# Cross attention scores from two float32r parts in 64-row tiles, with one maximum instruction for two heads

## The chip, the cores and the metric

The kernel is one program on one core of a Trainium2 chip. The metric is device time in microseconds (us) of one execution; the kernel before took 3319.63 us (median of three runs, 3304.61 to 3321.81).

## What is computed

Two decoder layers on x of shape (4, 512, 512), each with a mixer, a second mixer or cross attention on a context of shape (4, 512, 256), and a feed-forward part, each followed by a layer norm. Only the second layer's cross attention is touched. For each of 4 batches and 32 heads of 16 channels it is

```python
q, k, v = x @ Wq, *split(ctx @ Wkv)            # 512 tokens, 512 keys
q, k = apply_axial_rope(q, pos), apply_axial_rope(k, pos)
out = softmax(q @ k.T * 16 ** -0.5) @ v
x = layernorm(x + out @ Wout + bout)
```

in float32 accuracy.

## The kernel before

The program runs six stages one after the other; all engines go through them in the same order and meet by semaphores. The fifth stage is `Cross` (L3013). It works in 16 units, a unit being 8 heads of one batch (one block of 128 channels). The engines run a software pipeline written out by hand: `iterations()` gives i, and in iteration i the scores that go to the exponential belong to unit i, the scores for the maximum to unit i+1, and the projections of q, k and v to unit i+3. Each iteration has 32 steps m.

**The scores.** A product of float32 accuracy is made out of bfloat16 parts. After the rotation each of q and k is cut into three bfloat16 parts (`rope`, L3229: seven instructions on POOL for q and again for k; unit 0's k is cut on DVE). The parts go to memory (`d_parts`) and come back stacked, channel by channel, on 96 partitions (`sp_stack`, L3159: one store and six loads for each of q and k), so that one bfloat16 matmul over 96 rows adds the six products that matter. `pe_max` (L3335) makes a 128x512 tile of scores with it and DVE takes the row maximum, negated (L3545: one TENSOR_REDUCE per tile, 32 per unit). The maxima of half a unit are cut into three parts (`dve_parts`, L3520, four instructions), turned by TensorE (`mT`, L3314), copied by ACT (L3427) and put by three DMAs into rows 96 to 98 of Q (`sp_rows`, L3142), against rows of ones in K. `pe_exp` (L3347, matmul at L3355) then makes the transposed scores with the maximum already taken off, over 99 rows, and ACT takes the exponential (L3446: 32 per unit, 128x512). `pe_values` (L3358, matmuls at L3368) multiplies four heads' exponentials by the values in four 32-column tiles of TensorE, eight times a unit, once for every four exponentials.

**The order on TensorE** (`pe_all`, L3374) is, for each step m: one score matmul for the exponential, one for the maximum, the values if m % 4 is 1, and then one job from a list. `misc(i)` (L3078) gives that list: Rq and Rk (the projections of q and k, L3300), V (the projection of v, L3306), mT (L3314), turn (the attention output turned back, L3319, emptied on DVE by L3505 and L3508), aT (L3324), and at the end or start of a batch y (the output projection, four jobs, L3332, added and measured on DVE at L3512 and L269), xT (x turned, four jobs, L3286) and ang (angles, L3290, whose sines ACT makes with its own table, L3411).

**PSUM** has 8 banks: two for the exponential's scores (`rexp`), three for the maximum's (`rmax`), one for the values (`rav`), two in turn for the jobs of the list (`ring`). A job waits until the bank that it takes has been emptied.

**Queues.** DVE does, in step m, the maximum of step m, and after it the job that TensorE had in step m-2; ACT the exponential of step m and after it the job of step m-1. All DMAs of the stage are issued by SP in the order of `sp_all` (L3176): in iteration i the swap of q's channels, the rows of maxima, the swap of k's, after the second iteration of a batch the four stores of the batch before, the stack of q, the rows of the next unit's first half, the stack of k.

Of the kernel before, what the change touches and what calls it, by code (L numbers as in the profile page):

```python
# [12 lines left out]
F32 = mybir.dt.float32  # L13
# [6 lines left out]
P = 128  # L20
# [2992 lines left out]
class Cross(Stage):  # L3013
# [4 lines left out]
    name, pool_works, unrolled = "cross", True, True  # L3018
    H, DH = 32, 16
    CC = 2  # L3020
    Q_PARTS = (0, 1, 0, 2, 1, 0)
    K_PARTS = (0, 0, 1, 0, 1, 2)
    N = 6 * 16
# [6 lines left out]
    ONES = 1.0 + 0x3F80 / 2 ** 23  # L3030
    ONCE = ("cross_weights", "cross_late", "cross_ones", "cross_identb", "cross_half_pi")
# [6 lines left out]
    def __init__(self, io, carve, ps, x_in, x_out):  # L3038
# [26 lines left out]
        s.rav = Ring("cross_av", ps, 5, 1, [((u, g), "act") for u in range(s.UNITS) for g in range(2)])  # L3065
# [12 lines left out]
    def misc(self, i):  # L3078
# [3 lines left out]
        starts = (i + s.AHEAD + 1) % C == 0 and nb < B  # L3082
        if s.unit(f) is not None and i != -1:
            yield 1, ("Rq", f)
        if s.unit(i) is not None:
            yield 3, ("mT", i, 1)
        if s.unit(i - 1) is not None:
            yield 5, ("turn", i - 1, 1)
        if s.unit(f) is not None and i != -1:
            yield 7, ("Rk", f)  # L3090
        if s.unit(i - 1) is not None:
            yield 11, ("aT", i - 1)
        if s.unit(f) is not None:
            yield 15, ("V", f)
        ends = s.unit(i - 1) is not None and i % C == 0
        if starts:
            yield 17, ("ang", nb)
# [932 lines left out]
```

## Time and profile before

| | |
|---|---|
| median of three runs | 3319.63 us |
| the profiled execution | 3316.54 us, its span 3314.8 us |
| PE (TensorE matmul) busy | 2716.1 us, 82% of the span |
| DVE busy | 1958.6 us, 59% |
| ACT busy | 1433.1 us, 43% |
| POOL busy | 1177.7 us, 36% |
| score matmuls for the exponential, L3355 | 512, 198.4 us busy |
| score matmuls for the maximum, L3341 | 512, 201.4 us busy |
| maxima, L3545 | 512, 330.3 us busy |
| exponentials, L3446 | 512, 287.8 us busy |

Busy time of PE is that of overlapping records: a score matmul is shown 0.38 us long, and the next starts 0.22 us after it. A float32 matmul is two records. "Idle before" an instruction is put down to the instruction that ended it. Iterations can be told in the trace by Rq, the eight records of L3300, which stand at step 1.

### The profile page before, as it was taken

Reading aid. Unit: us, or ns where it says so; the run is one execution under the profiler, and the core shown is the slowest. Engines: PE = TensorE matmul, PEld = TensorE weight load, DVE = VectorE, ACT = ScalarE, POOL = GpSimd, SP = SyncE. Lnnn points to the kernel's source line nnn. Section 1 sums busy time; section 2 is a strip of 40 time slices with the busy share of each in tenths; the row PEclk is TensorE's granted clock in tenths of the full one; section 3 lists DMA queues with packets and bytes.
Section 4 is the critical chain, followed back from the end, with each engine's and each line's share of the span. In section 5 each row is a group of like instructions: output and inputs, shape, how many; then the busy total and the mean of one; then the engine's idle time right before and its main releaser. Section 6 shows DMA issues by size and latency. Waiting matters only on the chain.

```text
span 3314.8 us, 50665 instructions
## 1 busy us (share of the span) xinstructions
PE 2716.1 (82%) x20138; PEld 1454.0 (44%) x20154; DVE 1958.6 (59%) x3064; ACT 1433.1 (43%) x2577; POOL 1177.7 (36%) x1118
## 2 busy tenths in 40 slices
PE   5788888876677676589988898888768989899787
PEld 3565656553223232268845444444433333333244
DVE  3323232333689889956526566656655657476477
ACT  3232333320545555423426262635315546465555
POOL 0443333441566666600023625243243424241000
PEclk8888888887888888799998999998879989899999
DMA  2222222130330304032332424243155435252301
GB/s 87 71 59 62 52 78 60 47 87 14 121 116 13 127 26 140 13 140 95 137 108 86 128 90 125 93 122 130 39 117 107 105 69 112 61 109 53 118 26 39
DMA packets 209370, 280.04 MB, mean 84 GB/s; under 512 B 84640, under 2 KB 111680, under 8 KB 208240
## 3 DMA queue, kind: packets, MB, share of 16 engines
q1 hardware_dynamic: 209136, 276.81, 29.4%
q8 instruction: 160, 2.62, 0.3%
q14 instruction: 74, 0.61, 0.1%
HBM read 192.08 MB, written 59.12 MB: 76 GB/s over the span
## 4 chain that ended last, share of the span: by engine, by line
PE 39%; DVE 10%; issue 5%; ACT 4%; POOL 2%; DMA 1%; SPq 0%; ACTq 0%; DVEq 0%; POOLq 0%
PE ps L236 7%; PE ps L3368 4%; PE ps L1846 4%; PE ps L1857 4%; PE ps L3355 4%; PE ps L3341 3%; PE ps L3300 3%; PE ps L3332 2%; PE ps L2512 1%; ACT arena L3446 1%; PE ps L2520 1%; DVE arena L2775 1%; DVE arena L1434 1%; DMA arena<-arena 1%; DVE arena L2773 1%
## 5 line engine op out<-in xcount | busy, mean ns | idle before, releaser
L236 PE MATMUL ps<-arena 128*128 128x512 f32 (+3 forms) x1280 | 473.6, 522 | 18.3 <-ACT arena L2612 6.1
L3545 DVE TENSOR_REDUCE arena<-ps 128x1 f32<-128x512 f32 x512 | 330.3, 685 | 229.2 <-PE ps L3341 227.8
L3446 ACT ACTIVATE arena<-ps 128x512 f32<-128x512 f32 x512 | 287.8, 597 | 283.2 <-PE ps L3355 279.7
L1466 POOL TENSOR_TENSOR arena<-arena 128x1024 f32<-128x1024 f32 x128 | 311.0, 2430 | 192.9 <-DVE arena L1458 192.9
L1482 PE MATMUL ps<-arena 128*128 128x512 f32 x512 | 267.2, 662 | 55.8 <-POOL arena L1466 55.5
L1458 DVE TENSOR_TENSOR_SCAN arena<-ps,arena 128x1024 f32<-128x1024 f32 x128 | 291.5, 2278 | 32.9 <-ACT ps L1449 32.9
L236 PEld LDWEIGHTS ps<-arena 128*128 128x128 f32 (+2 forms) x1296 | 193.2, 154 | 252.3 <-issue 172.9
L1449 ACT ACTIVATE ps<-arena 128x511 f32<-128x511 f32 x256 | 165.1, 679 | 188.3 <-DVE arena L1458 188.1
L576 POOL TENSOR_TENSOR arena<-arena 128x31 f32<-128x31 f32 (+15 forms) x217 | 130.1, 600 | 324.2 <-DMA arena<-d_a 307.8
L3355 PE MATMUL ps<-arena 99*128 99x512 bf16 x512 | 198.4, 390 | 45.3 <-ACT arena L3446 33.4
L3341 PE MATMUL ps<-arena 96*128 96x512 bf16 x512 | 201.4, 395 | 19.1 <-issue 15.4
L1482 PEld LDWEIGHTS ps<-arena 128*128 128x128 f32 x512 | 104.6, 213 | 212.2 <-issue 125.7
L2276 POOL TENSOR_TENSOR arena<-arena 128x512 f32<-128x512 f32 x64 | 66.7, 1042 | 286.5 <-DVE arena L2928 286.5
L2654 ACT ACTIVATE arena<-arena 128x128 f32<-128x128 f32 x512 | 155.4, 388 | 8.4 <-PE ps L2570 8.4
L1434 DVE TENSOR_TENSOR arena<-ps,arena 128x1024 f32<-128x1024 f32 x128 | 154.4, 1206 | 1.6 <-PE ps L1482 0.7
L3238 POOL TENSOR_TENSOR arena<-arena 128x512 f32<-128x512 f32 x31 | 39.4, 1271 | 307.6 <-ACT arena L3419 307.4
L1084 DVE TENSOR_TENSOR arena<-ps,arena 128x256 f32<-128x256 f32 x120 | 51.0, 425 | 157.7 <-PE ps L777 157.7
L3368 PE MATMUL ps<-arena 128*32 128x512 f32 x1024 | 141.6, 626 | 1.0 <-ACT arena L3446 1.0
L3355 PEld LDWEIGHTS ps<-arena 99*128 99x128 bf16 x512 | 49.8, 98 | 197.4 <-ACT arena L3446 142.8
L1846 PE MATMUL ps<-sign,sign 128*128 128x512 f32 x512 | 122.5, 401 | 6.5 <-issue 6.5
L578 POOL TENSOR_TENSOR arena<-arena 128x31 f32<-128x31 f32 (+15 forms) x217 | 116.6, 537 | 17.0
L1857 PE MATMUL ps<-sign,sign 128*128 128x512 f32 x512 | 121.5, 396 | 0.0
(352 smaller groups left out, 5254.1 us busy)
## 6 DMA issues: line engine op xcount, KB each, us to landing
arena<-d_bc SPq DMA_DIRECT2D x32, 1024.0 KB, 5.7
arena<-d_x SPq DMA_DIRECT2D x24, 1024.0 KB, 6.8
arena<-d_parts SPq DMA_DIRECT2D x192, 128.0 KB, 4.6
d_x<-arena SPq DMA_DIRECT2D x64, 256.0 KB, 2.5
arena<-arena SPq DMA_DIRECT2D x128, 128.0 KB, 2.1
arena<-in_D_wlm SPq DMA_DIRECT2D x12, 1024.0 KB, 6.6
d_parts<-arena SPq DMA_DIRECT2D x32, 384.0 KB, 2.4
d_signs<-arena SPq DMA_DIRECT2D x32, 256.0 KB, 2.1
```

Of the source, the lines that this page charges most:

```text
L236: ins = pe.e.matmul(ps[:m, :n], lhsT(k), rhs(k), start=(k == 0), stop=(k == chunks - 1))
L1434: dve.e.tensor_tensor(s.h[:, i % s.HS].rearrange("p (w l) -> p w l", w=s.W), spread(s.ps[:, s.DTU, :], 1, s.W), s.bc[:, turn % s.SLOTS, 0] ...
L1458: dve.e.tensor_tensor_scan(h, s.dA[:, i % 2].rearrange("p w l -> p (w l)"), h, 0.0, ALU.mult, ALU.add).then_inc(*dve.up("scan_scanned"))
L1466: pool.e.tensor_tensor(h, h, s.bc[:, turn % s.SLOTS, 1], ALU.mult).then_inc(*pool.up("scan_hC"))
L1482: ins = pe.e.matmul(y, s.ident, s.h[:, i % s.HS, w * L:(w + 1) * L], start=False, stop=last)
L1846: ins = e.matmul(ps, s.up[m // 4][:, k, m % 4 * P:(m % 4 + 1) * P], s.xp[i][:, k, :], start=(k == i == 0), stop=(k == C - 1 and i == 1))
L1857: ins = e.matmul(ps, s.hp[i][:, m, t * P:(t + 1) * P], s.down[:, m, :], start=(m == i == 0), stop=(m == s.FC - 1 and i == 1))
L3341: pe.e.matmul(s.rmax.bank((u, m)), s.Qs[:s.N, slot, h, t * P:(t + 1) * P], s.Ks[:s.N, slot, h, :], start=True, stop=True).then_inc(*s.rmax ...
L3355: pe.e.matmul(s.rexp.bank((u, i)), s.Ks[:s.N + 3, slot, s.G * g + j, k * P:(k + 1) * P], s.Qs[:s.N + 3, slot, s.G * g + j, :], start=True, ...
L3368: ins = e.matmul(ps[32 * j:32 * j + 32, :], s.V[:, u % s.SLOTS, k, s.G * g + j, :], s.E[:, k % 2, j, :], start=(k == 0), stop=(k == s.KEYS ...
L3446: act.e.activation(s.E[:, k % 2, j], s.rexp.bank((u, i)), ACT.Exp).then_inc(*s.rexp.empty(act, (u, i)))
L3545: dve.e.tensor_reduce(s.mx[:, u % 2, t, h:h + 1], s.rmax.bank((u, m)), AX.X, ALU.max, negate=True).then_inc(*s.rmax.empty(dve, (u, m)))
```

## The change

- q and k are cut into two float32r parts instead of three bfloat16 parts (two instructions instead of four), and three products are added: 48 rows instead of 96. Even heads lie on partitions 0 to 47, odd heads on 64 to 111. Each load of `sp_stack` becomes two (six in all, as before, of the same 128 KB, in pieces of 2 KB instead of 1 KB); the store has 512 KB instead of 384 KB.
- A score matmul reads 48 rows (50 with the maxima) from row 0 or row 64, in float32r. TensorE issues two for the exponential, then two for the maximum, then the values, then the jobs.
- The two for the maximum fill two neighbouring banks and one TENSOR_REDUCE takes the maxima of both: 16 per unit, of 1024 columns.
- `rmax` has two slots of two banks, and `ring` one bank instead of two.
- The maxima are cut into two parts, by two instructions instead of four, and put in place by two DMAs instead of three. The rows of ones come from two DMAs ahead of SP's first swap instead of from four memsets on DVE.
- The jobs get other steps: xT at 9, 13, 23, 25; y at 27 and 29 and, in the next iteration, at 9 and 11 (after the last unit at 13, 15, 17, 19). The norm's square root moves from step 2 to 18, its scaling from step 4 to 20.

```diff
-    Q_PARTS = (0, 1, 0, 2, 1, 0)
-    K_PARTS = (0, 0, 1, 0, 1, 2)
-    N = 6 * 16
+    Q_PARTS = (0, 0, 1)
+    K_PARTS = (0, 1, 0)
+    N = 3 * 16
...
-        s.ring = Ring("cross", ps, 6, 2, [(name, s.EMPTIES[name[0]]) for i in s.iterations() for _, name in s.misc(i)])
+        s.ring = Ring("cross", ps, 7, 1, [(name, s.EMPTIES[name[0]]) for i in s.iterations() for _, name in s.misc(i)])
...
-        s.rmax = Ring("cross_max", ps, 2, 3, [((u, m), "dve") for u in range(s.UNITS) for m in range(s.STEPS)])
+        s.rmax = Ring("cross_max", ps, 2, 2, [((u, m), "dve") for u in range(s.UNITS) for m in range(0, s.STEPS, 2)], 2)
...
+            items += [(3, ("mT", i, 1)), (21, ("turn", i, 0))]
...
+            items += [(5, ("turn", i - 1, 1)), (13 if i > C and i % C == 1 else 11, ("aT", i - 1))]
...
+            items += [(at, ("xT", nb, t)) for t, at in enumerate((9, 13, 23, 25))]
+        ends = range(T) if i == s.UNITS else (0, 1) if i > 0 and i % C == 0 else (2, 3) if i > C and i % C == 1 else ()
+        at = (13, 15, 17, 19) if i == s.UNITS else (27, 29, 9, 11)
...
         for a, part in enumerate((s.Q_PARTS, s.K_PARTS)[w]):
-            sp.e.dma_start(dst[16 * a:16 * a + 16], d[:, :, part, :].rearrange("h d l -> d h l")).then_inc(*sp.up(f"cross_stack_{'qk'[w]}", 16))
+            for p in range(2):
+                at = 64 * p + 16 * a
+                sp.e.dma_start(dst[at:at + 16].bitcast(F32), d[p::2, :, part, :].rearrange("h d l -> d h l")).then_inc(*sp.up(f"cross_stack_{'qk'[w]}", 16))
...
-        hi, mid, lo = (s.parts[:, w, a] for a in range(3))
+        hi, lo = (s.parts[:, w, a] for a in range(2))
         e.tensor_copy(hi, s.m1[:, w]).then_inc(*eng.up_step("cross"))
         eng.e.wait_ge(*eng.at_step("cross"))
-        e.tensor_tensor(s.rest[:, w], s.m1[:, w], hi, ALU.subtract).then_inc(*eng.up_step("cross"))
-        eng.e.wait_ge(*eng.at_step("cross"))
-        e.tensor_copy(mid, s.rest[:, w]).then_inc(*eng.up_step("cross"))
-        eng.e.wait_ge(*eng.at_step("cross"))
-        e.tensor_tensor(lo, s.rest[:, w], mid, ALU.subtract).then_inc(*eng.up(f"cross_parts_{n}"))
+        e.tensor_tensor(lo, s.m1[:, w], hi.bitcast(F32), ALU.subtract).then_inc(*eng.up(f"cross_parts_{n}"))
...
         pe.e.wait_ge(*s.rmax.at_free(pe, (u, m)))
-        pe.e.matmul(s.rmax.bank((u, m)), s.Qs[:s.N, slot, h, t * P:(t + 1) * P], s.Ks[:s.N, slot, h, :],
-                    start=True, stop=True).then_inc(*s.rmax.fill(pe, (u, m)))
+        for p in range(2):
+            rows = slice(64 * p, 64 * p + s.N)
+            ins = pe.e.matmul(s.rmax.bank((u, m))[:, p, :], s.Qs[rows, slot, hh, t * P:(t + 1) * P], s.Ks[rows, slot, hh, :], start=True, stop=True)
+        ins.then_inc(*s.rmax.fill(pe, (u, m)))
...
-        pe.e.matmul(s.rexp.bank((u, i)), s.Ks[:s.N + 3, slot, s.G * g + j, k * P:(k + 1) * P], s.Qs[:s.N + 3, slot, s.G * g + j, :],
+        hh, p = 2 * g + j // 2, j % 2
+        rows = slice(64 * p, 64 * p + s.N + 2)
+        pe.e.matmul(s.rexp.bank((u, i)), s.Ks[rows, slot, hh, k * P:(k + 1) * P], s.Qs[rows, slot, hh, :],
...
-            for m in range(s.STEPS):
+            for m in range(1, s.STEPS, 2):
                 if s.unit(i) is not None:
+                    s.pe_exp(pe, i, m - 1)
                     s.pe_exp(pe, i, m)
                 if s.unit(i + 1) is not None:
-                    s.pe_max(pe, i + 1, m)
+                    s.pe_max(pe, i + 1, m - 1)
...
-                    dve.e.tensor_reduce(s.mx[:, u % 2, t, h:h + 1], s.rmax.bank((u, m)), AX.X, ALU.max, negate=True).then_inc(*s.rmax.empty(dve, (u, m)))
+                    if m % 2 == 0:
+                        h, t = m // (2 * T) * 2, m // 2 % T
+                        dve.e.wait_ge(*s.rmax.at_filled(dve, (u, m)))
+                        dve.e.tensor_reduce(s.mx[:, u % 2, t, h:h + 2], s.rmax.bank((u, m)), AX.X, ALU.max, negate=True).then_inc(*s.rmax.empty(dve, (u, m)))
```

## Rows read from the trace of the kernel before

**Rows 1.** Busy time by stretch, the whole stage: us, PE, PEld, DVE, ACT, POOL, clock, DMA

```profile
2414.83:3141.35 726.52, 636.94 (x3016) 237.80 (x3016) 441.06 (x806) 371.81 (x684) 244.86 (x234) 0.93 0.44 96
```

**Rows 2.** Chain that ended last, Rq of iterations 4 to 7, V of iteration 6

```profile
2637.26 3.64 PE ps L3300 x8
...
2703.99 3.64 PE ps L3300 x8
...
2743.30 3.64 PE ps L3300 x8
...
2760.22 1.79 PE ps L3306 x16
...
2777.29 3.64 PE ps L3300 x8
```

**Rows 3.** Timeline of PE, iteration 6, the matmuls that begin or end a round

```profile
2746.77 0.38 PE L3355 MATMUL ps<-arena 99*128 99x512 bf16 x1
...
2751.34 0.38 PE L3355 MATMUL ps<-arena 99*128 99x512 bf16 x1
...
2755.89 0.39 PE L3355 MATMUL ps<-arena 99*128 99x512 bf16 x1
...
2759.18 0.39 PE L3355 MATMUL ps<-arena 99*128 99x512 bf16 x1
...
2770.99 0.39 PE L3355 MATMUL ps<-arena 99*128 99x512 bf16 x1
...
2772.79 0.38 PE L3341 MATMUL ps<-arena 96*128 96x512 bf16 x1
2773.10 1.06 PE L3368 MATMUL ps<-arena 128*32 128x512 f32 x8
2774.09 0.39 PE L3355 MATMUL ps<-arena 99*128 99x512 bf16 x1
```

**Rows 4.** Timeline of ACT, the exponentials of the round at 2770.99

```profile
2771.42 2.22 ACT L3446 ACTIVATE arena<-ps 128x512 f32<-128x512 f32 x4 [0.88 <-PE ps L3355]
```

**Rows 5.** Timeline of DVE, iteration 6, emptying the job turn

```profile
2753.18 0.25 DVE L3505 RECIPROCAL arena<-ps 128x16 f32<-128x16 f32 x1
2753.46 0.43 DVE L3508 TENSOR_TENSOR arena<-ps,arena 128x256 f32<-128x256 f32 x1
```

**Rows 6.** Costliest groups of the page, DVE reading one and two banks

```profile
L3545 DVE TENSOR_REDUCE arena<-ps 128x1 f32<-128x512 f32 x512 | 330.3, 685 | 229.2 <-PE ps L3341 227.8
...
L1434 DVE TENSOR_TENSOR arena<-ps,arena 128x1024 f32<-128x1024 f32 x128 | 154.4, 1206 | 1.6 <-PE ps L1482 0.7
```

**Rows 7.** Lines L1857 (float32r) and L3355 (bfloat16): duration ns min/median/max

```profile
L1857 PEld LDWEIGHTS ps<-sign,sign x512: 187/188/192, 1468.4 to 1683.1; 128*128 128x128 f32 x171
L1857 PE MATMUL ps<-sign,sign x512: 389/396/483, 1468.6 to 1683.3; 128*128 128x512 f32 x171
...
L3355 PEld LDWEIGHTS ps<-arena x512: 96/97/152, 2489.9 to 3115.2; 99*128 99x128 bf16 x171
```

**Rows 8.** Timeline of PE, iteration 4, jobs that waited for DVE

```profile
2675.40 0.63 PE L3286 MATMUL ps<-arena 128*128 128x128 f32 x4 [1.50 <-DVE arena L3508]
...
2677.85 6.69 PE L3332 MATMUL ps<-arena 128*128 128x512 f32 x8 [1.38 <-DVE arena L3512]
```

**Rows 9.** Timeline of SP: stores of units 0 and 2, a stack, iteration 5's stores

```profile
2439.76 0.33 SPq L3166 DMA_DIRECT2D d_parts<-arena  x1
...
2474.06 0.37 SPq L3166 DMA_DIRECT2D d_parts<-arena  x1
2481.26 2.67 SPq L3174 DMA_DIRECT2D arena<-d_parts  x6
...
2722.74 2.09 SPq L3222 DMA_DIRECT2D d_x<-arena  x4
```

**Rows 10.** Timeline of PE, the first score matmul for the exponential

```profile
2489.96 0.59 PE L3355 MATMUL ps<-arena 99*128 99x512 bf16 x1 [8.39 <-issue]
```

**Rows 11.** DMA issues of the page, the stores of the parts: KB, us to landing

```profile
d_parts<-arena SPq DMA_DIRECT2D x32, 384.0 KB, 2.4
```

More of the change, by code:

```diff
@@ L3082, in misc @@
         starts = (i + s.AHEAD + 1) % C == 0 and nb < B
+        items = []
         if s.unit(f) is not None and i != -1:
-            yield 1, ("Rq", f)
+            items += [(1, ("Rq", f)), (7, ("Rk", f))]
         if s.unit(i) is not None:
-            yield 3, ("mT", i, 1)
+            items += [(3, ("mT", i, 1)), (21, ("turn", i, 0))]
         if s.unit(i - 1) is not None:
[L3088 to L3092, printed above, removed]
-        if s.unit(f) is not None:
-            yield 15, ("V", f)
-        ends = s.unit(i - 1) is not None and i % C == 0
-        if starts:
-            yield 17, ("ang", nb)
-        if s.unit(i + 1) is not None:
-            yield 19, ("mT", i + 1, 0)
-        if s.unit(i) is not None:
-            yield 21, ("turn", i, 0)
-        if i == -2:
-            yield 25, ("Rq", f + 1)
-            yield 27, ("Rk", f + 1)
-        for t in range(T):
-            if ends:
-                yield 22 + 2 * t, ("y", i // C - 1, t)
-            if starts:
-                yield 23 + 2 * t, ("xT", nb, t)
+            items += [(5, ("turn", i - 1, 1)), (13 if i > C and i % C == 1 else 11, ("aT", i - 1))]
+        if s.unit(f) is not None:
+            items.append((15, ("V", f)))
+        if s.unit(i + 1) is not None:
+            items.append((19, ("mT", i + 1, 0)))
+        if i == -2:
+            items += [(25, ("Rq", f + 1)), (27, ("Rk", f + 1))]
+        if starts:
+            items.append((17, ("ang", nb)))
+            items += [(at, ("xT", nb, t)) for t, at in enumerate((9, 13, 23, 25))]
+        ends = range(T) if i == s.UNITS else (0, 1) if i > 0 and i % C == 0 else (2, 3) if i > C and i % C == 1 else ()
+        at = (13, 15, 17, 19) if i == s.UNITS else (27, 29, 9, 11)
+        items += [(at[t], ("y", i // C - 1, t)) for t in ends]
+        return sorted(items)
     def sp_early(self, sp):
@@ L3480, in dve_before @@
         s, e = self, dve.e
+        e.memset(s.one[:2], 1.0).then_inc(*dve.up("cross_ones"))
         e.memset(s.V[:, :, :, :, 16:17], 1.0).then_inc(*dve.up("cross_ones"))
@@ L3483, in dve_before @@
         dve.e.wait_ge(*dve.at_all("cross_weights"))
-        e.tensor_copy(s.identb, s.ident).then_inc(*dve.up("cross_identb"))
-        for a in range(2):
-            e.memset(s.ones[:, a], s.ONES).then_inc(*dve.up("cross_ones"))
         s.rope(dve, 0, 1)
-        for a in range(2, s.SLOTS):
-            e.memset(s.ones[:, a], s.ONES).then_inc(*dve.up("cross_ones"))
     def dve_misc(self, dve, name):
```

78 lines of the change are left out of this document (40 added, 38 removed).

## The prediction

> **What bounds the kernel now.** I read the busy time of the whole stage first [rows 1]: 726.5 us, PE busy for 636.9, DVE 441.1, ACT 371.8. That looks like a stage bound by TensorE, which the change relieves. Then the chain [rows 2]: an iteration without jobs of a batch's end, from Rq to Rq, takes 2777.29 - 2743.30 = 34.0 us; iteration 4, which holds a batch's end and the next one's start, takes 66.7, and iteration 5 39.3. Then the timeline inside iteration 6 [rows 3]. I call a round what lies between two groups of values: four scores for the exponential, four for the maximum, eight records of values. A unit has eight. The round at 2770.99 has no job in it. Its eight score matmuls at 0.22 and the values at 1.08 (with 0.09 for going from one tile shape to the other: 2772.79 to 2773.10 is 0.31, not 0.22) are 2.84 us of work, but it takes 3.10. The rest is ACT: with two banks, the third score can start only when the first exponential is done. Its exponential starts at 2771.42 [rows 4], 0.43 after the score, and lasts 0.60; so the third score starts 1.08 after the first, the fourth 1.57 after it, then 0.22 for the maximum's score, 0.31, and 0.99 of values: 3.09. **The round is a loop between PE and ACT as much as PE work**, and the change leaves ACT's work and its two banks as they are.
>
> **A regular iteration, round by round.** Before, from [rows 3]: the round with mT and turn 4.57, with Rk 4.55, with aT 3.29, the three with V, with mT and turn, and without a job 2770.99 - 2759.18 = 11.81 together, the next 3.10, and the last, with Rq behind it, what is left of 34.0: 6.68.
>
> After, PE takes the scores in pairs. If the two halves of the array work side by side, a pair costs 0.22 us instead of 0.44. In a round without a job nothing is won: third and fourth score still start at 1.08 and 1.57, one pair for the maximum (0.22), 0.31, 0.99 make 3.1. Only a long job between the first and second pair hides ACT's loop. So:
> - V (1.79 us [rows 2]): before 8 x 0.22 + 1.08 + 1.79 = 4.63; after 4 x 0.22 + 1.08 + 1.79 + 0.1 for two more changes of tile shape = 3.9. Gain 0.7.
> - aT: 3.29 to 3.1. Gain 0.2.
> - mT and turn, both rounds: ACT's copies of the values and of Rq, which stand between its exponentials, set the pace; mT now waits for Rq's copy, as there is one bank, but that ends when the next exponential's bank comes free too. No gain, no loss.
> - **Rk loses.** It needs the one bank that turn holds. DVE empties turn only behind the maximum of the same step, so PE waits: the pair's scores for the maximum start at 0.22, DVE sees them at 0.64, reads two banks, then 0.25 and 0.43 [rows 5]. For the two-bank maximum the bounds are 0.69 (one bank) and 1.37 (twice that) [rows 6]; I take 1.2, after the 1024-column instruction of 1206 ns. Rk starts at about 2.5 where PE was free at 0.44. The same wait stands in the trace, shorter: xT waited 1.50 for turn's bank [rows 8]. The round becomes 2.5 + 1.72 + 0.1 + 0.44 + 1.08 = 5.9 instead of 4.55. Loss 1.3.
>
> Then the weights. A float32r load is 188 ns where a bfloat16 one is 97, and a float32r matmul whose load is not hidden is 483 ns instead of 389 [rows 7]: 0.09. Before, PE rarely had to wait with a bare load; after, the first score of a round (behind the values) and the third and fourth (released by ACT) do. Bounds: nothing, if the idle half is loaded ahead, to 0.27 a round (two loads of 0.09 and 0.1 by which the second of a pair starts late). I take 0.17 in six rounds: 1.0 a unit. A regular unit comes to 34.0 - 0.7 - 0.2 + 1.3 + 0.2 (shape changes at Rq) + 1.0 = **35.6**. Seven iterations (1, 2, 3, 6, 7, 10, 11): 7 x 1.6 = **+11**.
>
> The row says that four 32-column tiles do run at once (eight records in 0.99). The trace has no pair of row tiles 128 columns wide. The Trainium skill, page "TensorE: Matmul & The Clock Gate", section "Measured speedup vs the span model", says that tiles in different row groups start about 4 ns apart; by it a pair would cost one matmul plus 4 ns, and my 0.1 for the second one would fall away (0.8 a unit, 13 us over the stage). The page "TensorEngine Tiling (Array Packing)", section "PSUM Bottleneck", warns that tiling speeds up the matmuls but not the reading of PSUM; by that rule nothing is won here, and the round of 3.10 agrees.
>
> **Batch ends.** Iterations 4 and 5 take 106.0 now, 8 and 9 the same. That is 38.0 beyond two regular ones: four y of some 3.6 (14.4), four xT and ang, the two table loads of the sines and of the square root, waits for DVE of 1.50 and 1.38 [rows 8], and a y of 6.69 us [rows 8] where Rq, with as many records, has 3.64 [rows 2]. After, the same jobs stand in other steps: the waits behind turn and behind a first y stay (2.0 and up to 2.0 each), the 3 us of that slow y are likely to go, and so is 1 of the table loads, under which more of PE's work was waiting. 2 x 35.6 + 34 = 105. **-2** for both ends. Iteration 0, and 12 to 15, of which 12 and 13 end a batch without waiting much now: **+6**.
>
> **The store in SP's queue.** The norm's scaling moves to step 20; the four stores (2.09 us of issues [rows 9], 0.5 each) wait for it in SP's queue, and behind them stand the stack of q (0.4 to issue the store, 2.4 to land [rows 11], 2.67 for six loads [rows 9]) and the rows of maxima that the next unit's first exponential needs. Scaling ends some 10 us after step 18, the rows land some 9 later, PE is there after some 16: about 4 us of waiting in iterations 5 and 9: **+8**. Bounds 0 and 14.
>
> **The start.** Between the store of unit 0's q and that of unit 2's, four tensors pass in 34.3 us, and the first exponential's score starts at 2489.96 [rows 9, 10]. This stretch waits for DMAs: a store that lands in 2.4 us elsewhere [rows 11] took 7.2 (2474.06 to 2481.26). Loads in pieces of 2 KB need half as many packets; SP's own issues (0.4 for the store, 2.7 for the stack, 1.1 for two swaps at 0.5) and 2.4 for the store set a floor of 6.6 a tensor. I take 7.0 instead of 8.6: 6.3 us; 2 from two instructions fewer in POOL's first cut (about 1.0 each); 3.7 from the last store; 0.5 from one DMA fewer for the rows. **-13**, bounds -5 and -19. The two DMAs for the ones and their wait for DVE's memsets end before the first q is there: 0.
>
> **The end.** Four y with one bank instead of two: each waits for DVE to add and empty one bank, 0.69 as for a maximum over one bank [rows 6], and 0.1, three times: **+2**.
>
> DVE and POOL have fewer instructions, but neither sets the round: 0. Sum: 11 - 2 + 6 + 8 - 13 + 2 = +12. The sum stands against the profiled execution, 3316.5 us (span 3314.8), 3.1 below the median of three: **3328 us**.
>
> **Rivals.**
> - *The pairs run one after the other*, so that the halves do not share time and the change does not do what it says. Then in four rounds 0.66 and in eight more pairs 0.22 come on top: 4.4 a unit, 70 in all, 3398. For it: no such pair in the trace. Against it: the column tiles. Chance 0.10.
> - *The clock falls.* TensorE's granted clock is 0.93 over the stage [rows 1]; the y of 6.69 us stands behind idle stretches of 1.50 and 1.38 within 2.5 us of each other [rows 8], and has the pace of 1.2 GHz. After, PE idles 2 us at each Rk; if each Rk and its neighbours run at 1.2 instead of 2.4 GHz, 3.5 us in each of 12 units: 3370. Chance 0.12.
> - *The loads are hidden and the stores in time*, faster: 16 us of exposed loads and 8 of waiting go, and the start gives 19: 3298. The point is whether PE takes up the load for the free half while the other waits. Chance 0.22.
> - *PE work is the bound after all*, as the busy time suggests: 64 scores at 0.22 become 32 pairs, 6.6 us a unit, 3211 with all of it, 3260 with half. For it: PE busy for 636.9 of 726.5 us [rows 1]; against: those records overlap (0.38 long, 0.22 apart), and the round of 3.10. Chance 0.10.
> - My case, 3305 to 3350: 0.46.
>
> **Numbers.** A measurement of this kernel tells 0.5% (16.6 us) from no change. Faster than that (below 3300): 0.10 and half of 0.22 and some of my case's error, 0.28; slower (above 3333): 0.10, 0.12 and nearly half of my case, 0.41; the rest, 0.31, is no change. The range 3285 to 3385 leaves out the pairs in series and most of the PE case.
>
> **What the profile would show.** Pair right: the second score of a pair starts within 0.15 us of the first; wrong: 0.22 or more. Rk right: about 2 us of idle before L3300's four records, ended by DVE L3508. Loop right: a round without a job of 3.1 to 3.4; at 2.6 the PE case holds. Loads right: exponential scores 0.48 long where they waited for ACT. Store right: a score for the exponential waiting for the rows' DMA at the start of iterations 6 and 10. Start right: first exponential's score 62 us after the stage's start, not 75. Rq to Rq of 35 to 36 is the whole of it; 33 or less would make the prediction wrong.

## The result, and the profile after

The changed kernel takes 3433.93 us (median of 4 runs, 3427.3 to 3446.23) where the kernel before, run beside it, takes 3319.64 (4 runs, 3304.61 to 3321.81): a ratio of 1.0359 with a 95% interval of 1.0316 to 1.0401. The forecast of 3328 and its whole range were too low; that it would be slower had been given 0.41. Of all the executions behind this document one, of kernel 10 below, took 8468.76 us, and its ratio is taken without it. The profiled execution took 3446.23 us (span 3444.5), 12.3 above its median; that of before stood 3 below its own, so the traces differ by 129.7 us and the medians by 114.3.

The busy time of the stage, one answer of the windows view (the columns are those of [rows 1]):

```profile
2415.92:3271.00 855.08, 687.11 (x3016) 269.52 (x3016) 396.28 (x491) 375.02 (x684) 197.14 (x172) 0.84 0.37 87
```

The stage is 128.6 us longer than in [rows 1]: all of it is here. VectorE did less (396 against 441), which brought nothing; PE's busy time went up, although the two scores of a pair now overlap. The granted clock fell from 0.93 to 0.84, and the 1024 records of values, the same work as before, take 163.0 us on the page instead of 141.6. The page's groups of instructions say what PE then waited for:

```profile
L3542 DVE TENSOR_REDUCE cross<-ps 128x2 f32<-128x1024 f32 x256 | 311.8, 1223 | 386.4 <-PE ps L3340 385.7
L3450 ACT ACTIVATE cross<-ps 128x512 f32<-128x512 f32 x512 | 290.4, 596 | 393.6 <-PE ps L3357 392.4
L3357 PE MATMUL ps<-cross,cross 50*128 50x512 f32 x512 | 188.1, 555 | 46.3 <-ACT cross L3450 33.7
L3298 PE MATMUL ps<-cross,cross 128*128 128x512 f32 x192 | 114.5, 743 | 29.1 <-DVE cross L3508 24.4
```

The maximum over two banks takes 1223 ns, half a maximum each 612, where one bank took 685 [rows 6]. Neither DVE nor ACT is short of time: both idle some 390 us for PE. And Rk (L3298) waits 24.4 us for turn's bank. The waits of PE between 2500 and 3260 us (columns: us in total, times, longest):

```profile
PE ps L3298 <- DVE cross L3508: 24.4, 12, 2.0
PE ps L3310 <- ACT cross L3423: 19.2, 13, 1.5
PE ps L3328 <- DVE cross L3512: 10.8, 9, 1.9
PE ps L3310 <- ACT cross L3416: 10.8, 3, 3.6
```

The first is the wait that was forecast, in place and in size: twelve times 2.0 us. The sum has waits of y (L3328), for VectorE to add the y before it, at the batches' ends. It has none for mT (L3310), which waits for ScalarE to copy Rq out of the one bank, or for its sines. Now iteration 7 on PE's timeline; it is a regular one, as is iteration 6 of [rows 3]:

```profile
2835.69 0.50 PE L3357 MATMUL ps<-cross,cross 50*128 50x512 f32 x2
...
2837.94 0.60 PE L3310 MATMUL ps<-cross,cross 128*8 128x128 f32 x4 [1.51 <-ACT cross L3423]
...
2839.52 1.94 PE L3370 MATMUL ps<-cross,cross 128*32 128x512 f32 x8
2841.39 0.94 PE L3315 MATMUL ps<-cross,cross 128*128 128x128 f32 x4
2842.26 0.50 PE L3357 MATMUL ps<-cross,cross 50*128 50x512 f32 x2
2842.60 0.40 PE L3340 MATMUL ps<-cross,cross 48*128 48x512 f32 x2
2845.03 3.37 PE L3298 MATMUL ps<-cross,cross 128*128 128x512 f32 x4 [2.04 <-DVE cross L3508]
...
2850.21 1.07 PE L3357 MATMUL ps<-cross,cross 50*128 50x512 f32 x2
...
2862.95 0.50 PE L3357 MATMUL ps<-cross,cross 50*128 50x512 f32 x2
...
2864.13 0.98 PE L3357 MATMUL ps<-cross,cross 50*128 50x512 f32 x2 [0.45 <-ACT cross L3450]
...
2865.28 1.06 PE L3370 MATMUL ps<-cross,cross 128*32 128x512 f32 x8
2866.28 0.50 PE L3357 MATMUL ps<-cross,cross 50*128 50x512 f32 x2
```

Read three things. **The pairs do run side by side**: two scores for the exponential take 0.50 together, no longer than one of them does (the row below, the source view of L3357 for the pair at 2835.69), and the next pair starts 0.34 after them (2842.60 - 2842.26). **A round without a job** takes 2866.28 - 2862.95 = 3.33. **The clock**: behind the idle 1.51 the values take 1.94 instead of 1.06 and turn 0.94 instead of 0.66; behind the idle 2.04 the four records of Rk take 3.37, where they end in 1.96 at full rate: that is 1.2 instead of 2.4 GHz (granted clock 0.50 from 2839.52 to 2841.39 and 0.56 from 2845.03 to 2848.34, 1.00 from 2857.55 to 2858.55). The round of mT and turn takes 6.57 (2842.26 - 2835.69), the round of Rk 7.95. From Rq to Rq the iteration takes 40.9 us.

```profile
L3357 PE MATMUL ps<-cross,cross x2: 496/498/500, 2835.7 to 2835.7; 50*128 50x512 f32 x2
```

Its columns are the duration in ns (smallest, median, largest) and the first and last start.

Where the 128.6 us lie, from the starts of Rq in both traces (forecast in brackets): before the first Rq of iteration 0, 3.0 (-13); iterations 1, 2, 3, 6, 7, 10, 11, 285.6 - 238.0 = 47.6 (+11); iterations 4, 5, 8, 9, 243.9 - 212.1 = 31.8 (-2, and +8 for the store); iteration 0 and everything from the 12th on, 9.0 + 37.2 = 46.2 (+6 and +2).

### The profile page after: what moved, and what is told of

Same layout as the page of the kernel before. It is cut to its first block, busy times and chain, and to the rows that moved or that the text cites. A ratio compares the mean times of both kernels' runs of the same rounds, so it can differ in the third digit from the quotient of the medians.

```text
span 3444.5 us, 50265 instructions
## 1 busy us (share of the span) xinstructions
PE 2760.4 (80%) x20154; PEld 1478.7 (43%) x20154; DVE 1911.0 (55%) x2738; ACT 1436.7 (42%) x2577; POOL 1131.1 (33%) x1056
## 4 chain that ended last, share of the span: by engine, by line
PE 37%; DVE 9%; issue 5%; ACT 5%; DMA 2%; POOL 2%; SPq 1%; DVEq 0%; ACTq 0%; POOLq 0%
PE ps L236 7%; PE ps L3357 4%; PE ps L1846 4%; PE ps L1857 3%; PE ps L3370 3%; PE ps L3298 3%; PE ps L3328 2%; ACT cross L3450 1%; PE ps L3340 1%; DMA d_parts<-cross 1%; PE ps L2512 1%; PE ps L3304 1%; DVE arena L1434 1%; DVE arena L2775 1%; DMA arena<-arena 1%
## 5 line engine op out<-in xcount | busy, mean ns | idle before, releaser
L3542 DVE TENSOR_REDUCE cross<-ps 128x2 f32<-128x1024 f32 x256 | 311.8, 1223 | 386.4 <-PE ps L3340 385.7
L3450 ACT ACTIVATE cross<-ps 128x512 f32<-128x512 f32 x512 | 290.4, 596 | 393.6 <-PE ps L3357 392.4
L3357 PE MATMUL ps<-cross,cross 50*128 50x512 f32 x512 | 188.1, 555 | 46.3 <-ACT cross L3450 33.7
L3240 POOL TENSOR_TENSOR cross<-cross,cross 128x512 f32<-128x512 f32 x31 | 39.5, 1274 | 432.7 <-ACT cross L3423 432.7
L3357 PEld LDWEIGHTS ps<-cross,cross 50*128 50x128 f32 x512 | 71.9, 203 | 219.4 <-ACT cross L3450 122.1
L3370 PE MATMUL ps<-cross,cross 128*32 128x512 f32 x1024 | 163.0, 714 | 1.2 <-ACT cross L3450 1.2
L2276 POOL TENSOR_TENSOR arena<-arena 128x512 f32<-128x512 f32 x64 | 66.8, 1044 | 287.8 <-DVE arena L2928 287.8
L3340 PE MATMUL ps<-cross,cross 48*128 48x512 f32 x512 | 147.0, 469 | 15.5 <-issue 10.4
L3298 PE MATMUL ps<-cross,cross 128*128 128x512 f32 x192 | 114.5, 743 | 29.1 <-DVE cross L3508 24.4
L1846 PE MATMUL ps<-sign,sign 128*128 128x512 f32 x512 | 122.5, 401 | 6.5 <-issue 6.5
```

The source lines that it names most:

```text
L1846: ins = e.matmul(ps, s.up[m // 4][:, k, m % 4 * P:(m % 4 + 1) * P], s.xp[i][:, k, :], start=(k == i == 0), stop=(k == C - 1 and i == 1))
L3298: ins = e.matmul(ps, wt[:, k, cols], src[:, k, :], start=(k == 0), stop=(k == n - 1))
L3340: ins = pe.e.matmul(s.rmax.bank((u, m))[:, p, :], s.Qs[rows, slot, hh, t * P:(t + 1) * P], s.Ks[rows, slot, hh, :], start=True, stop=True)
L3357: pe.e.matmul(s.rexp.bank((u, i)), s.Ks[rows, slot, hh, k * P:(k + 1) * P], s.Qs[rows, slot, hh, :], start=True, stop=True).then_inc(*s.re ...
L3370: ins = e.matmul(ps[32 * j:32 * j + 32, :], s.V[:, u % s.SLOTS, k, s.G * g + j, :], s.E[:, k % 2, j, :], start=(k == 0), stop=(k == s.KEYS ...
L3450: act.e.activation(s.E[:, k % 2, j], s.rexp.bank((u, i)), ACT.Exp).then_inc(*s.rexp.empty(act, (u, i)))
```

## The experiments

Times are medians; each ratio is to the kernel before on the same chip, with its 95% interval. "Iteration" is Rq to Rq in a regular iteration (the 7th where nothing else is said): 34.0 before, 40.9 after.

**1. Rk before turn.**

```diff
-            items += [(1, ("Rq", f)), (7, ("Rk", f))]
+            items += [(1, ("Rq", f)), (5, ("Rk", f))]
...
-            items += [(5, ("turn", i - 1, 1)),
+            items += [(7, ("turn", i - 1, 1)),
```

> The changed kernel with Rk at step 5 and turn of the unit before at step 7, nothing else. Bank theory (the jobs' single bank makes PE wait 2.04 us for DVE before Rk, and the idle time brings the low clock, at which Rk takes 3.4 us and not 1.7): the wait before Rk goes, 12 units x (2.0 + about 1.7 + some of the low clock's rest) = 35 to 50 us less, about 3390. Tile theory (the float32r loads and the pairs cost it, waits are only where the time shows): the wait moves elsewhere, within 10 us of 3434.

Measured: 3419.19 us, ratio 1.0317 (1.0281 to 1.0353). The 2.0 us at Rk are gone, but turn now waits 1.0 us for ScalarE twelve times, and the iteration takes 36.6 to 38.8, about 3 less. The median is only 15 us below the changed kernel's, between what the two theories said, and the two intervals overlap. The wait at Rk is at most a part of the cause: where one bank is left, the next job waits instead.

**2. The maximum bank by bank.** Four single banks, one record a bank, one job bank as in the change.

```diff
-        s.rmax = Ring("cross_max", ps, 2, 2, [... for m in range(0, s.STEPS, 2)], 2)
+        s.rmax = Ring("cross_max", ps, 2, 4, [... for m in range(s.STEPS)])
```

> The changed kernel with the maximum taken bank by bank again (four single banks, 32 instructions of 512 columns per unit), the jobs' ring still one bank. Bank theory: no gain, DVE is a little later before turn is emptied (1.28 instead of 1.14 us), 0 to 5 us slower, 3434 to 3440. A theory that the two-bank maximum itself is what costs (PE gets its bank back later, DVE has longer instructions): 20 us or more faster.

Measured: 3433.76 us, ratio 1.0352 (1.0327 to 1.0377), the changed kernel's own time. **The two-bank instruction costs nothing and brings nothing that these intervals could show.** Its seven regular iterations take 37.8 to 41.2 us. The shortest, the 7th, has both waits and the full clock all the same:

```profile
2844.09 0.60 PE L3310 MATMUL ps<-cross,cross 128*8 128x128 f32 x4 [1.51 <-ACT cross L3423]
...
2849.80 1.96 PE L3298 MATMUL ps<-cross,cross 128*128 128x512 f32 x4 [2.08 <-DVE cross L3508]
```

and by the windows view (columns as in [rows 1]):

```profile
2838.21:2876.02 37.81, 32.51 (x180) 13.07 (x177) 23.56 (x41) 21.35 (x40) 16.38 (x14) 1.00 0.51 115
```

**3. Two job banks.** As 2, with three banks for the maximum, and the one that is left for the jobs.

```diff
-        s.ring = Ring("cross", ps, 7, 1, ...
+        s.ring = Ring("cross", ps, 6, 2, ...
```

> The changed kernel with the maximum bank by bank in three banks, as before, and the jobs' ring with two banks again; tiles, pairs and the new steps of the jobs stay. Bank theory: the waits before mT (1.51) and Rk (2.04) and the low clock behind them go, about 5 us in each of 13 units, and the start comes back: 3340 to 3370. Tile theory: 3420 or more.

Measured: 3356.04 us, ratio 1.0129 (1.0086 to 1.0171): **the bank that the two-bank maximum takes from the jobs is worth 78 us of the 114** (against 2 as well as against the change). Iteration 7 of this kernel on PE's timeline, Rq, mT, values, Rk and the next Rq:

```profile
2781.43 3.70 PE L3298 MATMUL ps<-cross,cross 128*128 128x512 f32 x8
...
2785.73 0.60 PE L3310 MATMUL ps<-cross,cross 128*8 128x128 f32 x4
...
2788.38 1.06 PE L3369 MATMUL ps<-cross,cross 128*32 128x512 f32 x8
...
2790.62 1.98 PE L3298 MATMUL ps<-cross,cross 128*128 128x512 f32 x4
...
2816.91 3.70 PE L3298 MATMUL ps<-cross,cross 128*128 128x512 f32 x8
```

No wait at mT or Rk, values in 1.06, Rk in 1.98, 35.48 us in all.

**4. The old parts in the change's order.** Six bf16 products and 96 rows as before; pairs, two-bank maximum, one job bank and steps as in the change.

```diff
+        for p in range(2):
+            ins = pe.e.matmul(s.rmax.bank((u, m))[:, p, :], s.Qs[:s.N, slot, h + p, t * P:(t + 1) * P], s.Ks[:s.N, slot, h + p, :], start=True, stop=True)
+        ins.then_inc(*s.rmax.fill(pe, (u, m)))
```

> The kernel before (three bfloat16 parts, 96 rows, no row tiles) with everything else of the change: pairs, two-bank maximum, one bank for the jobs, new steps. Bank theory: it has the same waits and pairs that cost 0.44 instead of 0.34, but loads of 0.10; it is slow too, 3420 to 3460. Tile theory: near the kernel before, 3320 to 3350.

Measured: 3409.78 us, ratio 1.0284 (1.0259 to 1.0308). Its iteration 7 has both waits, yet the clock holds:

```profile
2820.34 0.38 PE L3305 MATMUL ps<-arena 128*12 128x128 bf16 x4 [1.10 <-ACT arena L3413]
...
2821.63 1.07 PE L3360 MATMUL ps<-arena 128*32 128x512 f32 x8
...
2826.19 1.96 PE L3291 MATMUL ps<-arena 128*128 128x512 f32 x4 [2.03 <-DVE arena L3502]
```

The granted clock and the sums of that iteration, by the windows view (columns as in [rows 1]):

```profile
2814.66:2852.16 37.50, 33.59 (x180) 12.63 (x177) 22.83 (x29) 21.08 (x40) 19.40 (x18) 1.00 0.49 103
```

and of the same iteration of the changed kernel:

```profile
2832.06:2872.95 40.89, 35.71 (x180) 14.00 (x177) 22.23 (x25) 21.37 (x40) 16.38 (x14) 0.92 0.47 104
```

The clock is 1.00 against 0.92. The order, the banks and the steps are the same in both; the parts are not, and mT's gap is 1.10 here and 1.51 there. But the clock does not hold in every iteration: five of the seven regular ones take 37.5 at 1.00, and the 6th and the 10th, which have the same gaps of 1.10 and 2.03 and follow a batch's end, 40.1 and 40.2 at 0.93. In the changed kernel all seven are at 0.88 to 0.92. So the tiles add some 24 us to what order and bank cost.

**5 and 6. The kernel before with the change's steps, and then with one job bank.** 5 takes the change's `misc` (which step carries which job) and the norm at steps 18 and 20, and nothing else; 6 is 5 and this:

```diff
-        s.ring = Ring("cross", ps, 6, 2, ...
+        s.ring = Ring("cross", ps, 7, 1, ...
```

> The kernel before with the new steps of the jobs and of the norm alone (two job banks, single steps, bfloat16 parts). Store theory (the norm at steps 18 and 20 makes the stores and the rows behind them late, the y wait in other steps): 0 to 25 us slower than before. If the new steps are harmless or help the batch's end: within 10 us of 3317.

> As old_new_steps, and one bank for the jobs instead of two, nothing else (three banks for the maximum, single steps). Bank theory: this alone brings most of the loss, 50 to 80 us over old_new_steps. If pairs and two-bank maximum are needed for the loss: under 30 us.

Measured: 5 takes 3302.42 us (10 runs), ratio 0.9971 (0.9954 to 0.9988); 6 takes 3357.15, ratio 1.013 (1.0098 to 1.0162). **The new steps are worth 9 us by themselves, the one bank costs 55 in the old code.** In 6, where 5 has no such waits, iteration 7 shows:

```profile
2791.84 0.38 PE L3305 MATMUL ps<-arena 128*12 128x128 bf16 x4 [1.10 <-ACT arena L3410]
...
2797.31 1.96 PE L3291 MATMUL ps<-arena 128*128 128x512 f32 x4 [1.66 <-DVE arena L3499]
```

It takes 36.2 us instead of 34.0. Here too two of the seven regular iterations, the 1st and the 10th, have a lowered clock (37.9 us at 0.96, 38.9 at 0.93).

**7 and 8. The tiles with the old steps.** 7 is the change with two job banks, the maximum bank by bank, and the steps of before; 8 is 7 in the order of before, one score of each kind a step, the maximum's in the other half of the array:

```diff
-            for m in range(1, s.STEPS, 2):
+            for m in range(s.STEPS):
...
-        rows = slice(64 * (m % 2), 64 * (m % 2) + s.N)
+        rows = slice(64 * (1 - m % 2), 64 * (1 - m % 2) + s.N)
```

> The changed kernel with what cost it undone: maximum bank by bank in three banks, two job banks, the old steps of the jobs and the norm. Float32r tiles and the order in pairs stay. Bank and store theory: 3310 to 3335, near the kernel before. Tile theory (the exposed float32r loads cost a microsecond or two a unit): 3335 to 3356.

> As tiles_old_steps, in the old order of single steps, with the maximum's score always in the half of the array that the exponential's score does not use, so that the two can run together. If the side-by-side halves are worth anything in a stage paced by ACT's two banks: 3280 to 3315. If not: as tiles_old_steps, within 10 us.

Measured: 7 takes 3342.99 us, ratio 1.0076 (1.0051 to 1.01), iteration 35.4; 8 takes 3319.71 (10 runs), ratio 1.0021 (1.0003 to 1.0038), iteration 33.9. So among the tiles the order of pairs costs 1.5 us an iteration. The tiles without it stand where bf16 stood, 3319.71 us being in neither range that was expected of 8: no loss, and no gain from tiling either.

**9, 10, 11. Tiles and pairs, each alone on the new steps.** 9 is 8 with the steps of the change. 10 is 5 with the order of pairs and nothing else. 11 is the change with only the exponential's scores taken apart again.

```diff
-            for m in range(s.STEPS):
+            for m in range(1, s.STEPS, 2):
                 if s.unit(i) is not None:
+                    s.pe_exp(pe, i, m - 1)
                     s.pe_exp(pe, i, m)
```

> The 64-row tiles and the new steps of the jobs, but two banks for the jobs, the maximum bank by bank in three banks, and one exponential and one maximum score a step, the two in opposite halves of the array. Theory: the costs add up, the tiles alone cost some 7 us (3319.7 against the kernel before's 3312 on the earlier chip) and the new steps with two banks give some 9 back, so about 3305 to 3315, ratio 0.998 to 1.001, and below the 3356 of the same kernel in pairs. Rival: the tiles cannot bear the new steps (two float32r scores, then 2 us of values, then a bank wait), and it stays near 3340 or above.

> The kernel before with the new steps (3302 in the earlier run) and only the order of two exponential scores, two maximum scores and then the values and jobs of both steps; bf16 parts, two job banks, single maxima. Theory A: the order itself costs, as in the tiles (3343 against 3320 for pairs against single steps): 3320 to 3330, ratio 1.003 to 1.006, with waits of the exponential's score for ScalarE's exponential after each pair. Rival B: the order costs only where both scores of a pair share the rate of 64-row tiles: then 3300 to 3306, ratio 0.996 to 0.999.

> The changed kernel with one job bank and the two-bank maximum, but the two exponential scores of a pair apart: one, the pair of maximum scores, the other. Theory: the order of pairs costs its 20 to 25 us here too, so 3405 to 3415, ratio 1.027 to 1.031. Rival: with one bank the waits of Rk (2.0 us) and of mT (1.5 us) and the lowered clock behind them set the iteration whatever the order: 3428 to 3440, ratio 1.034 to 1.038.

Measured: 9 takes 3318.75 us (12 runs), ratio 1.0012 (0.9996 to 1.0028); 10 takes 3331.21, ratio 1.0044 (1.0024 to 1.0063); 11 takes 3427.51, ratio 1.034 (1.0314 to 1.0366). So **the order of pairs costs some 0.7% by itself** (10 against 5) and 1.1 us an iteration (35.1 against 34.0); 0.7 of it are scores that wait for an exponential, 1.6 us in all in iteration 7, 0.9 in that of 5. The tiles in single steps keep the iteration at 33.9; iteration 5 takes 49.7 us instead of 46.6 and the next 34.9 instead of 34.0, a part of the 0.4% between 9 and 5. 11 came out within the rival's ratios. Its regular iterations are shorter than the change's, 37.6 to 39.8 us at clocks of 0.87 to 0.95. The profiled executions differ by 17.6 us, but the changed kernel's stood 12.3 above its median; the medians differ by 6.4, and the intervals overlap. So with one bank no effect of the order is shown. How the halves share time, in iteration 7 of 9, the round of V:

```profile
2787.85 0.50 PE L3356 MATMUL ps<-cross,cross 50*128 50x512 f32 x1
2787.86 0.50 PE L3339 MATMUL ps<-cross,cross 48*128 48x512 f32 x1
2788.42 0.50 PE L3356 MATMUL ps<-cross,cross 50*128 50x512 f32 x1
2788.42 0.50 PE L3339 MATMUL ps<-cross,cross 48*128 48x512 f32 x1
2788.85 2.05 PE L3304 MATMUL ps<-cross,cross 128*128 128x128 f32 x16
```

An exponential's score and a maximum's start within 0.01 us here.

**12 and 13. Jobs four steps apart.** The change, and (13) kernel 5, with Rq 1, mT 5, turn 9, aT 13, Rk 17, mT 21, turn 25, V 29; ang 3, xT 7 to 19, y 23, 27 and 3, 7.

```diff
-            items += [(1, ("Rq", f)), (7, ("Rk", f))]
+            items += [(1, ("Rq", f)), (17, ("Rk", f))]
```

> The changed kernel whole (64-row tiles, pairs, two-bank maximum, one job bank), but with the regular jobs of an iteration four steps apart: Rq 1, mT 5, turn 9, aT 13, Rk 17, mT of the next unit 21, turn 25, V 29; ang, xT and y on the steps between. Theory: the one bank costs only because a job meets the copy-out of the one before; two rounds (6.6 us) lie between two jobs here, so the waits of mT for ScalarE (1.5), of Rk for VectorE (2.0) and most of the 1.2 GHz stretches go, and the kernel comes near the one with two job banks: regular iterations 35.5 to 37 and ratio 1.013 to 1.020. Rival: the waits only move (as when Rk and turn changed places), or the clock falls for another reason: regular iterations 39 to 41, ratio 1.028 to 1.036.

> The kernel before with its bf16 parts, single steps and two job banks, and the spaced jobs. Theory: with two banks no job waits for its bank (1.5 us in all in the new steps), so spacing changes nothing: as with the new steps, ratio 0.995 to 0.999. Rival: jobs spread over rounds even out what VectorE and ScalarE owe and the rounds shorten, or the later V and Rk delay a stage: under 0.994, or over 1.002.

Measured: 12 takes 3527.85 us, ratio 1.0633 (1.0597 to 1.0669), with iterations of 42.1 to 44.7 and one of 54.3; 13 takes 3355.87, ratio 1.0112 (1.0089 to 1.0135), with iterations of 37.7 to 40.5. Both of my cases for 12 missed, and the control says why in part: with two banks and the old parts, without a wait for a bank in iteration 7, spacing costs 3.7 us an iteration and more, 53 us in all. In 12 it cost 94. There the clock is lower as well: 0.69 in the iteration of 54.3, 0.90 to 0.96 in the others. All jobs had come to stand on steps that carry a values group. The timeline of 12, iteration 6:

```profile
2840.43 0.60 PE L3310 MATMUL ps<-cross,cross 128*8 128x128 f32 x4
2840.97 0.50 PE L3357 MATMUL ps<-cross,cross 50*128 50x512 f32 x2
2841.30 0.40 PE L3340 MATMUL ps<-cross,cross 48*128 48x512 f32 x2
2842.15 0.49 PE L3357 MATMUL ps<-cross,cross 50*128 50x512 f32 x1 [0.44 <-ACT cross L3450]
2843.09 0.49 PE L3357 MATMUL ps<-cross,cross 50*128 50x512 f32 x1 [0.45 <-ACT cross L3450]
```

mT did not wait, but behind it PE idles 0.44 and 0.45 for the exponentials of the half round that has no values. That a job put there would hide in that time is what the next run tries.

**14. Jobs apart, the long ones on steps without values.** The change with Rq 1, mT 5, turn 9, aT 13, Rk 15, V 19, mT 23, turn 27; ang 3, xT 7, 11, 17, 21, y 25, 29 and 3, 7.

```diff
-            items += [(1, ("Rq", f)), (7, ("Rk", f))]
+            items += [(1, ("Rq", f)), (15, ("Rk", f))]
```

> The changed kernel whole, one job bank, the jobs apart again, but the long ones on the steps that carry no values group: Rq 1, mT 5, turn 9, aT 13, Rk 15, V 19, mT of the next unit 23, turn 27. With all jobs on the steps of the values the iteration was 42.1 us though hardly a job waited for its bank: a job there adds its whole length (rounds of 4.3 us with an mT of 0.6), and the other half of the round idles for the exponentials of ScalarE. Theory: two things price a place, the bank and the half of the round; with both looked after the iteration is 36 to 38 us (40.9, less the waits of 1.5 and 2.0, less some 1.5 of the 1.2 GHz behind them, plus 0.9 for one more short job on a values step) and the ratio 1.015 to 1.025. Rival: only the place beside values counts, the bank waits are covered by idle time that is there anyway: 40 us or more, ratio 1.03 and up.

Measured: 3440.53 us, ratio 1.0417 (1.0372 to 1.0462), an interval that meets the changed kernel's. The regular iterations take 37.1 to 38.9 us in five of seven, close to the theory's 36 to 38, but 43.7 and 42.6 in the other two, whose granted clock is 0.80 and 0.82 (0.95 to 1.00 in the five), and the batch ends take what they did (iterations 4, 5, 8 and 9 together 242.4 instead of 243.9). In the profiles the iterations 0 to 11 take 571.9 us instead of 582.1; the medians show nothing of these 10, and the changed kernel's profile stood 12.3 above its median. Against 12 it is 87 us. By its ratio it was the rival's; the theory holds for those five iterations at most, and I have no version with one bank that keeps up with two. One reason stands in iteration 8:

```profile
2879.34 2.07 PE L3288 MATMUL ps<-cross,cross 32*128 32x512 f32 x2 [5.69 <-DMA cross<-in_E_posT]
```

ang (L3288), at step 3 instead of 17, waits for its positions. In the regular stretch mT no longer waits, Rk does, for aT's copy (iteration 7):

```profile
2844.43 0.66 PE L3315 MATMUL ps<-cross,cross 128*128 128x128 f32 x4
2845.02 0.50 PE L3357 MATMUL ps<-cross,cross 50*128 50x512 f32 x2
...
2850.70 1.96 PE L3298 MATMUL ps<-cross,cross 128*128 128x512 f32 x4 [1.02 <-ACT cross L3435]
```

Its 1.96 us are the pace of 2.4 GHz.

## Why the prediction was wrong

The regular iteration is the cleanest account, since each part was tried alone (iteration 7, with the granted clock in it):

| kernel | iteration, us | clock | ratio |
|---|---|---|---|
| before | 34.0 | 1.00 | 1 |
| + new steps (5) | 34.0 | 1.00 | 0.9971 |
| + single-step tiles, two banks (9) | 33.9 | 1.00 | 1.0012 |
| 5 + pairs (10) | 35.1 | 1.00 | 1.0044 |
| 5 + one job bank (6) | 36.2 | 1.00 | 1.013 |
| tiles + pairs, two banks (3) | 35.5 | 1.00 | 1.0129 |
| pairs + one bank, old parts (4) | 37.5 | 1.00 | 1.0284 |
| all, but the maximum bank by bank (2) | 37.8 | 1.00 | 1.0352 |
| all (the change) | 40.9 | 0.92 | 1.0359 |

The bank adds 2.2 and the pairs 1.1 to 34.0; together they give 37.5, nearly the sum. The tiles add 0.4 to the pairs (35.5 against 35.1). The sum of all would be 37.9, and that is what kernel 2 takes in its one regular iteration at full clock, 37.8. The 3.0 that are left are the clock's, and the rows name them: Rk 3.37 instead of 1.96, values 1.94 instead of 1.06, turn 0.94 instead of 0.66, 2.6 together. **The clock falls**, in all seven regular iterations of the change (0.88 to 0.92), in six of kernel 2, in two of kernels 4 and 6. The regular iterations before are all at 1.00.

So the sum failed in this: it put mT's wait at nothing, where the rows have 1.5 us thirteen times; it left the clock out, which took 3.0 us of a regular iteration; and for all that lies outside the seven regular iterations it had +1 (-2, +6, +8, -13, +2), where the trace has 81.0. Step by step, as the prediction put them:

- **"mT and turn, both rounds ... No gain, no loss": this step failed first.** It said that Rq's copy ends when the next exponential's bank comes free too. PE was ready for mT earlier: it idles 1.51 us, thirteen times in all. The round takes 6.57 instead of 4.57 [rows 3].
- **"Rk loses": mechanism and wait right (2.04 us), size off.** The round was put at 5.9 and takes 7.95 (2850.21 - 2842.26). Rk starts 2.77 after the round's first score instead of the 2.5 I took, and of the rest, 5.2 instead of 3.4, its own four records at the lowered clock are 1.4. In kernel 4, at full clock, the round takes 6.8 (first score to first score).
- **The clock rival was the likeliest companion of my own case, and I had weighed it as an alternative (0.12).** Its price, 3.5 us a unit, is near the 3.0 found. The row it rested on (a y of 6.69 us behind gaps of 1.50 and 1.38 [rows 8]) describes what my own step had just made: a gap of 2.0 in every iteration, to which the missed 1.5 came. The gaps do not decide it alone: kernel 4 has 1.10 and 2.03 in every regular iteration, with a clock of 1.00 in five and 0.93 in two, and kernel 2 has the tiles with 1.51 and 2.08 once at 1.00. The tiles make the fall the rule where it had been the exception. By which property, the longer gap at mT or the half-filled array, no run here tells.
- **"V: gain 0.7": no gain.** The round of V takes 4.85 (2858.55 - 2853.70), before 4.63. A pair for the exponential was taken as 0.22 and costs 0.34, and the second exponential's score of its first pair does not start beside the first; it waits for ACT. aT: 3.49, forecast 3.1.
- **The loop through ACT: right.** A round without a job takes 3.33, within the 3.1 to 3.4 named; ACT and DVE had time to spare. **Exposed loads: right in kind**, 0.49 to 0.50 for an exponential's score that starts alone, forecast 0.48; their price of 1.0 a unit was not measured by itself.
- **"Batch ends, -2": wrong; a second y was priced with its wait, but not with the clock.** Y waits behind y nine times, up to 1.9 us, aT behind y, and mT behind the sines. Iterations 4 and 5 take 121.0 instead of 106.0. The new steps alone bring them to 96.8 (kernel 5: 50.2 and 46.6), a gain that the sum did not have, one bank makes that 108.9, one bank and pairs 120.4. The stores behind the norm came as forecast in kind (a score waits for the rows' DMA), 1.55 us in iteration 5 and 1.89 in iteration 9 instead of 4. The first:

```profile
2788.01 0.80 PE L3357 MATMUL ps<-cross,cross 50*128 50x512 f32 x2 [1.55 <-DMA cross<-cross]
```

- **"The start, -13": wrong.** The first exponential's score stands 78.6 us behind the stage's start (2494.51), before 75.1. With pieces of 2 KB a tensor passed every 8.84 us, with those of 1 KB every 8.58. The four tensors moved 5.84 MB in 2851 packets (2444.91 to 2480.28), before 5.06 MB in 4014 (2439.76 to 2474.06): fewer packets, but more bytes, of which the wider store is 0.5 MB. While the loads ran, the rate was the same: 134 to 146 GB/s in four stretches of 4 us, before 131 to 143. Most of the loss lies ahead of that: the first store leaves 29.0 us behind the stage's start instead of 24.9, and already the first Rq stands at 10.7 instead of 7.9. xT and ang wait there for ScalarE to empty the one bank, four times, and so do the projections behind them:

```profile
2426.64 6.54 PE L3298 MATMUL ps<-cross,cross 128*128 128x512 f32 x8 [0.78 <-ACT cross L3411]
2433.96 1.96 PE L3298 MATMUL ps<-cross,cross 128*128 128x512 f32 x4 [0.78 <-ACT cross L3423]
2439.43 3.67 PE L3298 MATMUL ps<-cross,cross 128*128 128x512 f32 x8 [0.78 <-ACT cross L3427]
```

- **"The end, +2": the mechanism right**, three y each waiting 0.78 (taken 0.79), but the first runs at 1.2 GHz: 19.8 us for the four, before 15.4.

```profile
3242.80 6.35 PE L3328 MATMUL ps<-cross,cross 128*128 128x512 f32 x8 [0.78 <-ACT cross L3435]
3249.93 3.70 PE L3328 MATMUL ps<-cross,cross 128*128 128x512 f32 x8 [0.78 <-DVE cross L3512]
```

- **The rivals.** The pairs are not in series, so that rival is out. So is the one with hidden loads (0.49 to 0.50 above), and the one that PE's work is the bound: its 6.6 us a unit (by its own figures 32 x 0.22 = 7.0) never came. The tiles at their best (33.9) leave the iteration as it was. The Trainium skill, page "TensorEngine Tiling (Array Packing)", section "PSUM Bottleneck", says that tiling speeds up TensorE but not the emptying of PSUM; these runs agree. By the Trainium skill, page "TensorE: Matmul & The Clock Gate", section "Measured speedup vs the span model", a pack of tiles spans one matmul and about 4 ns for each further tile. The trace agrees: in kernel 9 the starts are at most 0.01 us apart, and in the change the pair at 2835.69 fills 0.50 with two scores of 496 and 500 ns. So the 0.1 by which my bounds let the second score start late is not there. What the pair costs above 0.22 lies before the next one: that starts 0.34 behind.

- **"Iteration 0, and 12 to 15: +6": wrong, 9.0 and, with the end, 37.2.** The clock is low here too: 0.82 in iteration 0 (before 0.91), and 0.50 in a whole stretch of 24.4 us in iterations 13 and 14, from mT to mT, which took 13.4 before:

```profile
3152.98:3177.37 24.39, 21.01 (x74) 7.00 (x72) 12.74 (x17) 12.44 (x22) 0.00 (x0) 0.50 0.11 44
```

A round without a job takes 4.98 us in it (3166.26 - 3161.28) instead of 3.33. The last unit, from its last mT to the first y, takes 34.9 at 0.74 instead of 26.9 at 0.99. The square root of the norm, which the change moves to step 18, stands at the start of the 24.4 us with two table loads of 1.28 on ScalarE, and a score waits 2.51 for an exponential. It is not the whole cause: kernel 5 has the same root there and takes 19.1 at 0.82, and kernel 7, whose root is at step 2, has such a stretch too, 23.2 at 0.55. Both have what the change has in part: 5 the steps, 7 the pairs of half-height scores.

What stays open: why the clock stays low so long with pairs of half-height scores, and the rest of the 46 us of iteration 0 and of everything from the 12th on, which was not taken apart one by one.

## What to carry to other kernels

A wider operand in PSUM is paid by whoever owned the bank: before taking one, list every job that shares what is left, and for each the engine that copies the job before it out, not only the wait that looks worst. Price waits that the change adds together with the clock they may cost: here the clock cost 3.0 us of a regular iteration's 6.9. And when engines are in a loop, a saving on PE's records is worth nothing outside the places where PE is late: the tiles at their best gave 0.1 us of an iteration here. The place of the jobs counted for more: all of them on the values' steps cost 3.7 us an iteration (13 against 5).

## What the runs showed of the hardware

- Two scores of 50 rows and 512 float32r columns in the two halves of the array fill 0.50 us together, as long as one of them, and the next pair starts 0.34 behind. Two bf16 scores of full height take 0.22 each. So such a pair, at the start of a round, saved 0.10 of 0.44, where half had been counted on.
- A load of float32r weights for 50 rows of the array lasts 182 to 183 ns (smallest and median of L3357 in the change), one for 48 rows 182 to 187 (L3340), one for all 128 rows 187 to 188 [rows 7]: half the height saves next to nothing.
- A maximum over 1024 columns in two banks takes 1223 ns, 0.15 less than two of one bank, and nothing came of it.
- Gaps of 1.5 and 2.0 us in an iteration of pairs of half-height scores brought 1.2 GHz in all seven regular iterations of the change (granted clock 0.88 to 0.92) and in six of seven of kernel 2. Gaps of 1.1 and 2.0 in one of full-height scores did so in two of seven (kernel 4: 0.93, else 1.00).
- Loads into 16 partitions moved 134 to 146 GB/s in pieces of 2 KB and 131 to 143 in pieces of 1 KB.
